# A second cross attention worked by quads of batches, with split products for keys and output projection, and keys spread a round ahead in the other attentions

## What is computed

```
x = x + tanh(g_xattn[0]) * L0_xattn(layernorm(x), ctx)     # 16 heads of 8
x = x + tanh(g_ffn[0])   * L0_ffn(layernorm(x))            # 64 experts of 64, 6 chosen, and a shared one
x = x + tanh(g_xattn[1]) * L1_xattn(layernorm(x), ctx)     # 16 heads of 64
x = x + tanh(g_ffn[1])   * L1_ffn(layernorm(x))            # causal latent attention, then 8 experts of 256, 2 chosen

def L1_xattn(hidden, encoder, Wq, Wk, Wv, Wo, bo):
    q, k, v = hidden @ Wq, encoder @ Wk, encoder @ Wv      # 16 heads of 64
    probs = softmax(einsum('bhsd,bhkd->bhsk', q, k) / 8, axis=-1)
    out = einsum('bhsk,bhkd->bhsd', probs, v)              # heads back side by side: 1024 wide
    return out @ Wo + bo
```

## Time and profile before

| | |
|---|---|
| median of 3 runs | 2061.7 us (2058.45 to 2063.37) |
| the profiled execution | 2061.8 us, span 2060.0 us |
| busy share of the span | PE 87%, PEld 68%, DVE 73%, ACT 54%, POOL 57% |
| mean granted TensorE clock | 0.928 of 2.4 GHz |
| second cross attention | 950 to 1420 us |
| first cross attention, its rounds | 76 to 290 us |
| causal attention, its rounds | 1478 to 1720 us |

### The profile page before, as it was taken

The page is one execution under the profiler, slowest core; times in us unless marked ns, Lnnn a source line. Parts: engine busy times, 40 slices in busy tenths (PEclk is TensorE's granted clock), DMA queues, the critical chain, the costliest instruction groups (busy, mean ns, idle before and its releaser), DMA issues. The chain is left out here.

```text
span 2060.0 us, 40382 instructions
## 1 busy us (share of the span) xinstructions
PE 1802.4 (87%) x12276; PEld 1398.8 (68%) x12306; DVE 1510.3 (73%) x3109; ACT 1112.8 (54%) x2864; POOL 1177.6 (57%) x1241
## 2 busy tenths in 40 slices
PE   3678767799999999986999999997778887799998
PEld 2355546588888888864888888885444444588886
DVE  5698868677787787777666666666668886677876
ACT  1366645555555555543666666664346565555554
POOL 3666637467776777654333333334767773677764
PEclk9799976799999999985999999998879997699999
DMA  5111100455565555410000000000000000212222
GB/s 122 46 44 40 42 25 11 113 137 138 144 144 145 125 148 145 128 60 3 5 4 3 4 4 3 4 3 1 0 1 1 0 0 16 60 61 83 81 63 71
DMA packets 99991, 114.77 MB, mean 56 GB/s; under 512 B 18448, under 2 KB 55504, under 8 KB 99888
## 3 DMA queue, kind: packets, MB, share of 16 engines
q1 hardware_dynamic: 96960, 112.14, 20.6%
q10 hardware_dynamic: 2928, 1.39, 0.3%
HBM read 101.82 MB, written 3.28 MB: 51 GB/s over the span
## 5 line engine op out<-in xcount | busy, mean ns | idle before, releaser
L76 POOL TENSOR_TENSOR b_moe_hid_low<-b_moe_hid,b_moe_hid_high 128x512 fp32r<-128x512 f32 x256 | 331.9, 1296 | 172.0 <-ACT b_moe_hid_high L1027 168.4
L1033 ACT ACTIVATE bank<-bank 128x512 f32<-128x512 f32 x384 | 223.5, 582 | 341.3 <-PE bank L83 341.3
L1729 POOL TENSOR_TENSOR c_prob<-c_prob,c_recip 128x480 f32<-128x480 f32 x128 | 126.3, 987 | 294.0 <-DVE c_recip L1877 294.0
L1835 ACT ACTIVATE c_prob<-bank,c_shift 128x120 f32<-128x120 f32 x512 | 177.9, 360 | 169.7 <-DVE c_shift L1869 169.7
L1058 DVE TENSOR_TENSOR b_moe_gu<-bank,XC 128x512 f32<-128x512 f32 x256 | 176.7, 690 | 114.8 <-PE bank L83 99.0
L76 POOL TENSOR_TENSOR e_moe_hid_low<-e_moe_hid,e_moe_hid_high 128x512 fp32r<-128x512 f32 x128 | 165.9, 1296 | 83.5 <-ACT e_moe_hid_high L1027 82.8
L71 DVE CAST c_ts_high<-bank 128x480 fp32r<-128x480 f32 x128 | 84.2, 658 | 153.2 <-PE bank L1760 153.2
L1063 DVE TENSOR_TENSOR b_moe_hid<-bank,b_moe_gu 128x512 f32<-128x512 f32 x256 | 177.0, 691 | 8.9 <-POOL b_moe_hid_low L76 0.3
L1027 ACT ACTIVATE b_moe_hid_high<-b_moe_hid 128x512 fp32r<-128x512 f32 x256 | 159.7, 624 | 9.8 <-DVE b_moe_hid L1063 9.0
L1760 PE MATMUL bank<-c_cs,mT 96*128 96x120 f32 x1024 | 142.2, 283 | 6.2 <-POOL c_wvp_low L76 4.8
L1760 PEld LDWEIGHTS bank<-c_cs,mT 96*128 96x128 f32 x1024 | 132.8, 196 | 20.8 <-DVE c_ts_low L76 9.7
(11 more groups left out here) (372 smaller groups left out, 5490.4 us busy)
## 6 DMA issues: line engine op xcount, KB each, us to landing
XC<-b_comb SPq DMA_DIRECT2D x256, 256.0 KB, 4.3
XC<-e_comb SPq DMA_DIRECT2D x64, 256.0 KB, 3.1
X<-in_x SPq DMA_DIRECT2D x4, 512.0 KB, 9.1
a_att_qs_high<-XC SPq DMA_DIRECT2D x32, 64.0 KB, 1.8
a_att_qs_low<-a_Q_low SPq DMA_DIRECT2D x32, 64.0 KB, 1.9
a_att_ks_high<-a_K_high SPq DMA_DIRECT2D x32, 64.0 KB, 1.9
a_att_ks_low<-a_K_low SPq DMA_DIRECT2D x32, 64.0 KB, 1.9
b_moe_w_gate<-in_b_wgT SPq DMA_DIRECT2D x8, 256.0 KB, 2.8
```

The source lines that it names most:

```text
L76: return eng.tensor_tensor(low.bitcast(F32R), x, high, ALU.subtract)
L1033: act.activation(gate_b[j % 4][:], gate_b[j % 4][:], ACT.Silu).then_inc(s_silu, 1)
L1729: pool.tensor_tensor(prob[k][:], prob[k][:], recip[:, k, :].unsqueeze(2).broadcast_to([P, HG, NKV]), ALU.mult).then_inc(s_norm, 1)
L1835: i = act.activation(prob[k][:, h, :], score_b[g % 2][:, h * NKV:(h + 1) * NKV], ACT.Exp, bias=shift[:, k, h:h + 1], accum_out=sums[:, k, ...
```

## The change

Stage c is written anew. A quad is four batches; a block is one quad with one group of four heads, and a slot is one batch of a block, again 128 slots, but the batches of one block follow each other. The context of a quad is loaded at once. **Keys** of a block are made a block ahead, one head per slot for all four batches (480 columns), as a split product, for which `mT` gets a high and a low part; VectorE splits the result into `ts`, which now holds a block. **Values** come per two slots as two products of 256 columns. **Scores** read `XT` directly (the copies `xs` are gone). The transposes have **one** bank instead of two (`turn_b`), since the projection got bank 7. **Heads** are split (ScalarE high part, VectorE low part) and **projected** once a block over four batches as two split products of 512 columns that add up over the quad's four blocks into a transposed sum; per quad ScalarE copies that sum, TensorE transposes it back in four, VectorE adds it to `X` in one instruction. The probabilities lie in `XC`. The loops are no longer hardware loops but written out.

```diff
@@ attend_both_ways, GpSimd
+                    def spread_keys(b, v):
+                        if clamp:
+                            pool.wait_ge(s_place[v], (b - v) * 16 + 64)
+                        else:
+                            low_parts(b, v)
+                            pool.wait_ge(s_low, b + 1)
+                        wait(pool, s_second, b - 1)
...
+                    spread_keys(0, 0)
+
                     def body(b, v):
                         u = v % 2
+                        if has(b + 1):
+                            spread_keys(b + 1, (v + 1) % 4)
                         if has(b):
-                            if clamp:
-                                pool.wait_ge(s_place[v], (b - v) * 16 + 64)
-                            else:
-                                low_parts(b, v)
-                                pool.wait_ge(s_low, b + 1)
-                            wait(pool, s_second, b - 1)
...
                             wait(pool, s_first, b + 1)
@@ stage c
-        key_b, side_b, score_b, turn_b, out_b = bank[0], bank[1], bank[2:4], bank[4:6], bank[6:8]
+        key_b, value_b, score_b, turn_b, out_b, y_b = bank[0], bank[1], bank[2:4], bank[4], bank[5:7], bank[7]
@@ TensorE
+                def keys(n):
+
+                    m, h = n // 4 + 1, n % 4
...
+                    wait(pe, s_kcopy, n + 4)
+                    split_product(pe, key_b[:, 0:4 * NKV], [t[:, HG * (m % NG) + h, :] for t in mTs],
+                                  [t[:].rearrange("p b k -> p (b k)") for t in csp[(m // NG) % 2]]).then_inc(s_key, 1)
+
+                def scores(n):
+                    m, j = n // 4, n % 4
+                    b = 4 * (n // 16) + j
+                    pe.wait_ge(s_kcopy, 4 * m + 4)
+                    wait(pe, s_exp, n - 1)
...
+                def turn(n):
+                    pe.wait_ge(s_norm, n + 1)
+                    wait(pe, s_copied, n)
...
+                for n in range(FIRST, LAST):
+                    keys(n)
+                    if 0 <= n < SLOTS:
+                        scores(n)
+                    if 0 <= n - 4 < SLOTS:
+                        turn(n - 4)
+                    if 0 <= n - 6 < SLOTS:
+                        heads(n - 6)
+                    if n % 2 == 1 and 0 <= n < SLOTS:
+                        values(n // 2)
+                    if n % 4 == 0 and 0 <= n // 4 - 3 < BLOCKS:
+                        project(n // 4 - 3)
+                    if n % 16 == 10 and 0 <= n // 16 - 1 < NQ:
+                        turn_sum(n // 16 - 1)
@@ ScalarE
+                for n in range(FIRST, LAST):
+                    i = n // 2 - 1
+                    if n % 2 == 0 and 0 <= i < SLOTS // 2:
...
+                        act.activation(vs[m % 2][:, 2 * half:2 * half + 2, :],
...
+                    r = n - 5
+                    if 0 <= r < SLOTS:
+                        act.wait_ge(s_turn, r + 1)
+                        wait(act, s_pv, r - 1)
+                        act.activation(probT[r % 2][:], turn_b[0:NKV, :], ACT.Copy).then_inc(s_copied, 1)
+                    if 0 <= n < SLOTS:
                         act.wait_ge(s_shift, n + 1)
...
+                    i = (n - 8) // 2
+                    if n % 2 == 0 and 0 <= i < SLOTS // 2:
...
+                        act.activation(oT[m % 2][0][:, :, 256 * half:256 * half + 256].bitcast(F32R),
+                                       out_b[i % 2].rearrange("p (k t) -> p k t", k=2), ACT.Copy).then_inc(s_ohigh, 1)
@@ VectorE
+                for n in range(FIRST, LAST):
+                    m, h = n // 4 + 1, n % 4
+                    if m < BLOCKS:
+                        dve.wait_ge(s_key, n + 5)
...
+                        keep_high(dve, high, key_b[:, 0:4 * NKV]).then_inc(s_kh, 1)
+                        dve.wait_ge(s_kh, n + 5)
+                        keep_low(dve, low, key_b[:, 0:4 * NKV], high).then_inc(s_kcopy, 1)
+                    if 0 <= n < SLOTS:
                         dve.wait_ge(s_score, n + 1)
                         wait(dve, s_exp, n - 7)
...
```

More of the change, by code:

```diff
@@ L1694, in _ @@
             def _(sp):
[L1695 to L1704 removed]
+                for qd in range(NQ):
+                    wait(sp, s_cl, qd)
+                    sp.dma_start(raw[:], ctxT[4 * qd:4 * qd + 4].rearrange("b e t -> e b t")).then_inc(s_cs, 16)
@@ new lines, in heads @@
+                def heads(n):
+                    m, j = n // 4, n % 4
+                    pe.wait_ge(s_copied, n + 1)
+                    if j % 2 == 0:
+                        pe.wait_ge(s_vcopy, n // 2 + 1)
+                        wait(pe, s_olow, n // 2 - 1)
+                    o = out_b[(n // 2) % 2].rearrange("p (k b t) -> p k b t", k=2, b=2)
+                    for h in range(HG):
+                        rows = slice(C_DH * (h % 2), C_DH * (h % 2) + C_DH)
+                        t = pe.matmul(o[rows, h // 2, j % 2, :], vs[m % 2][:, j, C_DH * h:C_DH * h + C_DH],
+                                      probT[n % 2][:, h * P:(h + 1) * P], start=True, stop=True)
+                    t.then_inc(s_pv, 1)
@@ new lines, in values @@
+                def values(i):
+                    m, half = i // 2, i % 2
+                    columns = slice(HG * C_DH * (m % NG), HG * C_DH * (m % NG + 1))
+                    wait(pe, s_vcopy, i)
+                    if i == 0:
+                        pe.wait_ge(s_wl, 1)
+                    for j in range(2):
+                        t = split_product(pe, value_b[0:NKV, j * HG * C_DH:(j + 1) * HG * C_DH],
+                                          [t[:, 2 * half + j, :] for t in csp[(m // NG) % 2]],
+                                          [t[:, columns] for t in wvp])
+                    t.then_inc(s_v, 1)
@@ new lines, in project @@
+                def project(m):
+                    pe.wait_ge(s_olow, 2 * m + 2)
+                    if m == 0:
+                        pe.wait_ge(s_ol, 1)
+                    g = m % NG
+                    if g == 0:
+                        wait(pe, s_add, m // NG)
+                    for k in range(2):
+                        t = split_product(pe, y_b[:], [t[:, 2 * g + k, :] for t in wos], [t[:, k, :] for t in oT[m % 2]],
+                                          start=(g + k == 0), stop=(g == NG - 1 and k == 1))
+                    t.then_inc(s_y, 1)
```

299 lines of the change are left out of this document (116 added, 183 removed).

## The result

The changed kernel takes 2089.85 us (median of 4 runs, 2086.73 to 2098.0) beside 2062.53 us for the kernel before (4 runs, 2058.45 to 2065.47): ratio 1.0133, 95% interval 1.0117 to 1.0149. It is 27 us slower.

The account below looks back on a forecast made before the run. TensorE's list (14.23 us per four slots) bounds the second cross attention, then the ring (15.0). 2061.8 + 35 (ring 21, ends 4, start 10) - 10 (causal attention) = 2087 us, range 2040 to 2106.

Parts of the forecast that it names:

- the ring: Second cross attention: transposes wait for the single bank's copy, behind exponentials, maximum and key split; 15.0 us per four slots.
- The ring's length: Second cross attention: 5.48 us from keys to transposes, then transposes, heads, values; two slots at least 7.49 us.
- Even slots 14.6, shorter: Second cross attention: the ring counted by even slots, with the projection, 14.6 us per four slots against 15.0.
- odd above all: Second cross attention: waits of 0.5 to 1.5 us ahead of the transposes in most slots, chiefly odd ones.
- The size between the ends: Second cross attention, first maximum to last addition: 21 us from the ring plus 4 for fill and tail.
- fill and tail: Second cross attention's ends: filling 5 more, last slots without keys 3 back, tail 2 more; together 4 us.
- TensorE's own list: Second cross attention: TensorE's work alone, 13.7 us per four slots after the change against 14.23 before.
- the first rival: Second cross attention: the ring does not bind, 13.7 per four slots; 2047 us, down to 2030 with shorter passes; chance 0.20.
- Start: Second cross attention: block 0's four heads made ahead of slot 0, 3.2 us each, first maximum 10 us later.
- The rival of the longer time at 1.2 GHz: Key rounds: 10 to 20 us more at half clock add 8 to 15 us, 2100; chance 0.12.
- Keys a round ahead: Causal attention: 0.39 us less per round, 25 rounds, 10 us, the exponential then limiting; first attention 0.

Follow-up runs that it names:

- copy_early: Changed kernel, but ScalarE copies the turned probabilities ahead of the same slot's exponentials, with three `c_probT` tiles instead of two: 2025.02 us, ratio 0.9813.
- heads_behind: Changed kernel, but ScalarE copies the heads' sums in the odd slot, behind the copy that frees the turned bank: 2085.11 us, ratio 1.0105.
- before_keys_ahead: Kernel before, with only the keys' spreading on GpSimd moved a round ahead in the first and causal attention: 2052.59 us, ratio 0.9947.
- after_keys_old: Changed kernel, with GpSimd spreading keys in the batch's own round again in the first and causal attention: 2098.36 us, ratio 1.0161.

## Why the prediction was right, point by point

- **The bound moves from TensorE's list to the ring.** Shown: opened, it gives 65 us; lengthened by 0.48 a slot, it costs 29.5; put alone into the old kernel, it costs 55. The rule quoted from the Trainium skill (Perfetto Trace Analysis, section Matmuls) that product groups should rotate through banks agrees with these runs. What copy_early adds: one bank was enough here once its emptying was ordered right behind its filling (12.90 us a group, no wait at the transposes).
- **The ring's length.** The step from keys to transposes was put at 5.48 and is 5.39; transposes 0.55 and heads 0.59 for 0.53 and 0.58; values 0.81 for 0.9. Two slots 7.35 for 7.49, four 14.70 for 15.0. "Even slots 14.6, shorter" holds: heads_behind leaves that side in charge and stays at 14.67, so both sides are in effect equal. The forecast said "odd above all"; the waits ahead of the transposes are of one size on both sides (0.63 and 0.58 us at 1222.51 and 1225.79), and in the other two slots of a group TensorE stood only 0.26 and 0.33.
- **The size between the ends.** 24.3 us against the 25 forecast, but partly by luck: 0.47 a group for 0.75 makes 13 instead of 21 over 28 groups; the group with the turned sum, 15.55, adds 0.85 seven times, 6, and the ring's sum had neither the sum's copy on ScalarE nor its turn on TensorE (only 0.13 in TensorE's list); 5 remain for fill and tail, forecast 4. Two errors nearly cancelled.
- **TensorE's own list was over-sized**, without harm to the result: 12.90 for 13.7. Keys and scores take 0.64 and 0.66 for 0.74, values 0.81 for 0.9 (near the lower of its bounds), the projection 1.50 for 1.4. It does harm the first rival, whose 2047 should have been near 2025, below even the 2030 given for shorter passes: copy_early shows what the change is worth where the ring does not bind.
- **Start.** 7.3 us for 10 in this profile: the key loops take 3.0 for 3.2, and the first keys come at 952.91 for 955. With the scatter said above (954.1 to 958.6 elsewhere), the 10 is as good a number.
- **Clock.** The rival of the longer time at 1.2 GHz is out in this stage: granted 0.50 over the first 20 us as before, 0.95 over the next 40, then 1.00 (before: 1.00 from 970 on).
- **Keys a round ahead.** 10.1 us in the trace for 10; the exponential has become the limit, as said. In the first attention the last maximum of the rounds moved by 0.8 us (276.8 to 276.0): 0, as said.
- By the Trainium skill's rule to work on the most contended engine (Perfetto Trace Analysis, section Identifying the Most-Contended Engine) the change should have won: it took 1.3 us of 14.23 from TensorE. It lost nevertheless: the bank given up for it had kept the other engines' steps off TensorE's path, and its loss alone costs the old kernel 55 us.

## What to carry to other kernels

Before a buffer is taken from a rotation, write down the ring that it closes: from its refill, through every in-order engine, back to the refill, each step from a row, and compare the sum with the period of the fullest engine times the slots it spans. Where the ring is longer, first look for an order in which the emptying instruction stands right behind the filling one and ahead of unrelated work of its engine; here that and one more tile in on-chip memory were worth 65 us. Put the rare instructions into the sum too: one copy and one turn in 16 slots made 6 us here. Work that sits in a ring counts in full though its engine is one third idle; and of two interleaved rings of nearly one length, shortening one shows little (7 and 1.5 us here, 23 together).

## What was not expected of the hardware

- **The first split pass behind fp32 products costs 0.1 us more.** Keys, in copy_early: 0.21 from first to second pass behind values (1224.78 to 1224.99), 0.32 behind heads:

```profile
1221.44 0.48 PE L81 MATMUL bank<-c_csp_high,c_mT_high 96*128 96x480 f32 x1
...
1221.76 0.38 PE L82 MATMUL bank<-c_csp_high,c_mT_low 96*128 96x480 f32 x1
```

In the old kernel every score product stood behind fp32 keys and took 0.74; with split keys ahead it takes 0.66. The weight loads differ in the same way: behind values they begin 0.12 ahead of the pass (1224.66), behind heads together with it (1221.44). Which property of the product ahead does it was not tested. Passes of 256 columns follow each other by 0.12 us (1218.43, 1218.55, 1218.67), half of the 0.23 of 512 columns. So cutting a product in two by columns cost 0.02 a pair here.

- **A small VectorE instruction ends with the GpSimd instruction beside it.** `a_att_mz` (128 x 16) takes 285 ns before and 736 with the keys spread a round ahead (27 instances from 100 to 270 us; 710 and 286 in before_keys_ahead and after_keys_old). In the changed kernel it now falls beside GpSimd's spreading, and ends with it:

```profile
170.84 0.99 POOL L489 TENSOR_TENSOR a_att_kd_low<-a_att_ks_low,headsel 128x480 fp32r<-128x480 f32 x1
171.11 0.74 DVE L696 TENSOR_SCALAR a_att_mz<-a_att_negmax,a_att_limit 128x16 fp32r<-128x16 f32 x1
```

GpSimd ends at 171.83 and VectorE at 171.85; at the next instance at 178.00 and 178.03. The Trainium skill (SBUF — State Buffer, on the port pair that VectorE and GpSimd share) describes such a pair as locked for a whole instruction while the other engine blocks, for VectorE instructions in a two-port mode or with two inputs from SBUF. The common end in these rows fits a lock; that VectorE ends 0.02 later and not its own 0.29 later does not follow from it. That the port is the cause was not tested, nor whether this instruction is of the kind named, and the longer instruction costs nothing here: the attention ends 0.8 us earlier.
